# Diagonal products over both chunks of a unit in one matmul, with the results sorted on three engines

## What is computed

```python
x   = xBC[..., :D_INNER]                  # 64 heads x 16
Bm  = xBC[..., D_INNER:D_INNER + 512]     # 8 groups x 64 states
Cm  = xBC[..., D_INNER + 512:]
A_cum  = cumsum(A)                        # within a chunk
Lm     = exp(segsum(A))                   # decay from token z to token s of a chunk
Y_diag = einsum('bcshn,bczhn,bhcsz,bczhp->bcshp', Cm, Bm, Lm, X)
states = einsum('bcshn,bhcs,bcshp->bchpn', Bm, decay_states, X)
Y_off  = einsum('bcshn,bchpn,bhcs->bcshp', Cm, states, exp(A_cum))
y      = Y_diag + Y_off
out    = ((y + D * x / dt) * silu(z + z_bias)) @ out_proj_w.T
```

## Time and profile before

| | us |
|---|---|
| three runs | 672.77, 673.68, 674.39 |
| median | 673.68 |
| the profiled execution, whole | 675.71 |
| its span, first to last instruction | 674.0 |

### The profile page before, as it was taken

The page is one execution under the profiler, slowest core; times in us unless marked ns, Lnnn a source line. Parts: engine busy times, 40 slices in busy tenths (PEclk is TensorE's granted clock), DMA queues, the critical chain, the costliest instruction groups (busy, mean ns, idle before and its releaser), DMA issues.

```text
span 674.0 us, 21311 instructions
## 1 busy us (share of the span) xinstructions
PE 625.0 (93%) x8371; PEld 490.9 (73%) x8371; DVE 520.8 (77%) x947; ACT 383.7 (57%) x834; POOL 357.9 (53%) x416
## 2 busy tenths in 40 slices
PE   3786978999999999999999999999987989999995
PEld 1654856777877777778777777877866767888884
DVE  5799589788777786887878877787789466677766
ACT  3876453545756545665655565656665527665555
POOL 5775211535554554753644556356566746767652
PEclk9798788999999999999999999999998999999999
DMA  8743111142421231312122163221414634454411
GB/s 287 209 171 116 45 38 52 58 159 62 138 72 36 72 110 61 111 56 97 49 94 71 53 179 113 90 85 52 131 56 125 219 119 140 139 159 125 126 48 62
DMA packets 61914, 70.52 MB, mean 105 GB/s; under 512 B 13972, under 2 KB 33460, under 8 KB 61816
## 3 DMA queue, kind: packets, MB, share of 16 engines
q1 hardware_dynamic: 61816, 69.17, 32.2%
HBM read 54.45 MB, written 14.70 MB: 103 GB/s over the span
## 4 chain that ended last, share of the span: by engine, by line
PE 72%; DVE 12%; issue 4%; POOL 4%; ACT 3%; DMA 2%; SPq 1%; DVEq 0%; POOLq 0%; ACTq 0%
PE bank L1196 34%; PE bank L1963 11%; PE pair L1261 7%; PE bank L1205 4%; PE bank L1996 3%; PE pair L1234 3%; DVE m_cv L1447 2%; PE bank L1291 2%; PE bank L1214 2%; PE pair L1247 2%; DMA p_wa_raw<-in_L_attn_in_proj_w_dram 2%; DVE m_M L1477 1%; POOL h_lo L428 1%; DVE chain L589 1%; DVE chain L596 1%
## 5 line engine op out<-in xcount | busy, mean ns | idle before, releaser
L1447 DVE SCALAR_TENSOR_TENSOR m_cv<-bank,gpc,m_cv 128x511 f32<-128x511 f32 (+2 forms) x192 | 143.5, 748 | 35.5 <-ACT m_cv L1354 31.0
L1196 PE MATMUL bank<-h_hi,w_hi 128*128 128x512 f32 x384 | 160.8, 419 | 4.3 <-DVE m_xs L1468 2.1
L1196 PE MATMUL bank<-h_hi,w_lo 128*128 128x512 f32 x384 | 152.6, 397 | 0.0
L1196 PE MATMUL bank<-h_lo,w_hi 128*128 128x512 f32 x384 | 152.4, 397 | 0.0
L1592 POOL TENSOR_TENSOR m_S<-m_S,m_cd 128x128 f32<-128x128 f32 x96 | 39.9, 416 | 158.1 <-DVE m_S L1510 81.7
L1354 ACT ACTIVATE m_cv<-bank,gpc 128x512 f32<-128x512 f32 x96 | 72.0, 750 | 67.0 <-PE bank L1196 67.0
L1196 PEld LDWEIGHTS bank<-h_hi,w_hi 128*128 128x128 f32 x384 | 73.8, 192 | 24.0 <-issue 5.9
L1196 PEld LDWEIGHTS bank<-h_hi,w_lo 128*128 128x128 f32 x384 | 73.2, 191 | 16.9 <-issue 0.2
L1196 PEld LDWEIGHTS bank<-h_lo,w_hi 128*128 128x128 f32 x384 | 73.9, 192 | 13.7
L1366 ACT ACTIVATE m_M<-bank 128x512 f32<-128x512 f32 x128 | 76.2, 595 | 12.9 <-PE bank L1205 11.3
L1477 DVE TENSOR_TENSOR m_M<-m_M,pair 128x512 f32<-128x512 f32 x128 | 81.8, 680 | 0.2 <-issue 0.2
(11 more groups left out here) (184 smaller groups left out, 1271.9 us busy)
## 6 DMA issues: line engine op xcount, KB each, us to landing
m_ea<-ea_scratch SPq DMA_DIRECT2D x32, 256.0 KB
m_dd<-dd_scratch SPq DMA_DIRECT2D x32, 256.0 KB
y_scratch<-m_t SPq DMA_DIRECT2D x16, 512.0 KB, 3.4
h_lo_place<-y_scratch SPq DMA_DIRECT2D x16, 512.0 KB, 4.9
p_wm<-in_L_wmod_dram SPq DMA_DIRECT2D x6, 1024.0 KB, 7.7
m_wraw<-in_L_attn_in_proj_w_dram SPq DMA_DIRECT2D x18, 256.0 KB, 3.1
w_lo_place<-in_L_attn_input__dram SPq DMA_DIRECT2D x16, 256.0 KB, 5.0
out_dram<-t_o SPq DMA_DIRECT2D x16, 256.0 KB, 2.3
```

Source lines behind the costliest of these rows:

```text
L1196: ins = pe.matmul(A[k % 3][:, :], w[:, t, kc, :], h[:, n % NB, kc, :], start=(m == 0), stop=(m == 11))
L1447: ins = dve.scalar_tensor_tensor(out=cv[:, k % 3, lag:], in0=A[k % 3][:, 0:L - lag], scalar=s.gpc[:, gp, o:o + 1], in1=cv[:, k % 3, lag:], ...
```

## The change

A diagonal product now takes all 128 partitions, that is both chunks of a unit at once. Since the two chunks must not be added, a product handles head h of chunk 0 and the neighbouring head of the other parity of chunk 1: `Xp` holds x of chunk 1 at swapped places (`placed`), and the decay rows of chunk 1 are loaded with even and odd heads swapped, from a second scratch tensor `asw_d` in which SyncE stores them that way. So 16 products of 128 rows, 32 columns of weights and 64 moving columns take the place of 32 products of 64 rows. Their results go to columns 128 to 383 of `GB` (`OWN`), beside the turned B. In them even heads have their chunks in swapped order, odd heads in the right one. They are sorted by three engines: ScalarE copies them with the chunks swapped, times 1 on partitions of even heads and 0 on others (`even_heads`, a new instruction in slot 1), VectorE's `collect` adds them times the opposite mask, and GpSimd adds the even copy to `y1` (`add_even`, new). The masks (`s.parity`) are made once by six small GpSimd instructions. `spread` is two instructions of 64 partitions each, `weigh` two of 256 columns, the zeros included.

New waits: `turn_b(u)` waits for the collect of unit u-2, `diagonal(u)` for the copy of the B of unit u+1, `collect` for the even copy, and the sum of a step for `add_even`. `turn_b` moves ahead of the projection half of slot 3, and `exponent(u, 0)` ahead of `spread(u)`.

```diff
             def turn_b(u):
                 wait(pe, bt_read, u)
+                wait(pe, y1_done, u - 1)
                 pe.transpose(GB[:, 0:P], Bt[:, n % 2, tok(u)], s.ident[:, :]).then_inc(bt_done, 1)
...
             def diagonal(u):
                 wait(pe, y1_done, u)
+                pe.wait_ge(bt_read, min(u + 2, NU))
                 pe.wait_ge(s_new, n_new(u, 1))
                 pe.wait_ge(m_done, 2 * u + 2)
                 pe.wait_ge(xp_done, u + 1)
                 for q in range(2):
-                    for e in range(2):
+                    for a in range(2):
                         for j in range(4):
-                            for c in range(2):
-                                half, h = slice(64 * c, 64 * c + 64), 2 * j + e
-                                ins = pe.matmul(YS[32 * j:32 * j + 32, c, q * Q:(q + 1) * Q], Xp[half, u % 2, HG * q + h, :],
-                                                M[half, u % 2, q, h * Q:(h + 1) * Q], start=(e == 0), stop=(e == 1))
+                            h = 2 * j + a
+                            ins = pe.matmul(OWN[32 * j:32 * j + 32, q, (1 - a) * Q:(2 - a) * Q], Xp[:, u % 2, HG * q + h, :],
+                                            M[:, u % 2, q, h * Q:(h + 1) * Q], start=True, stop=True)
                 ins.then_inc(yd_done, 1)
...
                     if sl == 3 and u < NU:
                         decay(u, 1)
+                        turn_b(u)
                     if slot + 8 in PART_AT:
                         project(*PART_AT[slot + 8])
...
-                    if sl == 3 and u < NU:
-                        turn_b(u)
...
+            def even_heads(u):
+                act.wait_ge(yd_done, u + 1)
+                wait(act, y_added, u - 1)
+                act.activation(own_even[u % 2][:, :, :].rearrange("p q (c s) -> p q c s", c=2),
+                               OWN.rearrange("p q (c s) -> p q c s", c=2)[:, :, ::-1, :], ACT.Copy, scale=s.parity[:, 0:1]).then_inc(even_done, 1)
...
+                    if sl == 1 and v >= 0:
+                        even_heads(v)
...
                     if sl == 2 and u < NU:
+                        exponent(u, 0)
                         spread(u)
-                        exponent(u, 0)
...
-                dve.tensor_tensor(dst[:, first:, :, :], own[:, first:, :, :], dst[:, first:, :, :], ALU.add).then_inc(y1_done, 1)
+                dve.scalar_tensor_tensor(out=dst[:, :, first:], in0=OWN[:, :, first:], scalar=odd, in1=dst[:, :, first:],
+                                         op0=ALU.mult, op1=ALU.add).then_inc(y1_done, 1)
...
-                pool.tensor_tensor(Xw[:, :, :].rearrange("p q (j e d) -> p (q j) e d", e=2, d=HD), src, w, ALU.mult).then_inc(xw_done, 1)
+                for a in range(2):
+                    src, dst = (t[:, a::2, :].rearrange("p j (e d) -> p j e d", e=2) for t in (Xp[:, u % 2, :, :], Xw[:, :, :]))
+                    ins = pool.tensor_tensor(dst, src, w, ALU.mult)
+                ins.then_inc(xw_done, 1)
...
+            def add_even(u):
+                pool.wait_ge(y1_done, u + 1)
+                pool.wait_ge(even_done, u + 1)
+                y = y1[:, n % 2, :, tok(u)]
+                pool.tensor_tensor(y, y, own_even[u % 2][:, :, :], ALU.add).then_inc(y_added, 1)
...
                 if v + 2 < NU:
                     weigh(v + 2)
                     fade(v + 2, 0)
+                if v >= 0:
+                    add_even(v)
```

97 lines of the change are left out of this document (67 added, 30 removed).

## The result

The changed kernel takes **681.61 us** (median of four runs, 679.96 to 684.11) where the kernel before takes 673.22 beside it (671.30 to 674.39). The ratio is 1.0113, with a 95% interval of 1.0082 to 1.0143: slower by 1.1% (the two medians by themselves give 1.0125), where 666.0 was forecast. The profiled execution took 682.06 us with a span of 680.3.

What follows compares the result with a forecast made beforehand. TensorE's own stream was taken to bound the long middle (99.64 of 100 us busy). Terms -11.5 + 3.8 - 0.7 + 0.5 = -7.9 us from the 673.7 median gave 665.8, said as 666; range 660 to 673.

Steps and rivals of the forecast that it cites:

- The diagonal group: TensorE's diagonal products at a unit's head: 0.79 to 0.58 us, 0.21 less in 55 units, 11.5 us gained.
- Rivals B: Diagonal group shorter still, only its columns count: 0.44 us a unit, 661 us in all; chance 0.13.
- E: No gain in the diagonal group: a 128-row record costs twice a 64-row one, 0.79 stays, 677 us; chance 0.04.
- F: Weight loads show in each of the diagonal group's eight rounds, 0.13 us each, 725 us in all; chance 0.03.
- SyncE: Six small loads a unit instead of four, issued two units ahead (13 us): hidden, nothing counted, below 1 us otherwise.
- GpSimd: 1.2 us more a unit, 52% to 70% busy; TensorE waits 0.54 for the weighting in seven units, 3.8 us lost.
- The new wait of the turn of B on the collect: TensorE's turn of B waits for the collect of unit u-2: 1.4 us to spare in unit 29, nothing counted.
- The copy of B and VectorE's chain: Before the diagonal: chain about level, 0.5 us counted over the run; ScalarE's copy of B level, nothing counted.
- rivals C: VectorE's chain before the diagonal takes the gain back: odd units return about 0.2 us each, 671 to 672; chance 0.12.
- D: Diagonal waits for ScalarE's late copy of B: at 0.3 us a unit 16.5 us, 682 in all; chance 0.06.
- the sign that the prediction had named for itself: Unit 28 to unit 29, start to start, takes 6.46 us; wrong if it stays at 6.67 with a new idle stretch.
- The exponential ahead of the spread: ScalarE's first exponential no longer behind the 0.38 us spread, so TensorE's second decay product waits less: 0.7 us gained.

Runs made afterwards that it cites:

- run 1: Changed kernel with the six decay-row loads queued ahead of the store and scale loads on SyncE in a step's first unit; 1.0021 of the kernel before.
- run 5: Kernel before with only GpSimd's additional work put in from unit 8 on (second weighting, even-heads-sized add into a spare buffer); 1.0048, median 678.68 us.
- run 2: Changed kernel with GpSimd's new work taken away (half the weighting, one column of the even heads' sum), a test only; 0.9957 of the kernel before.
- run 4: Kernel of run 1 with, on GpSimd in a step's first unit, the weighting and fade ahead of the first gating; 0.9954 of the kernel before.
- run 8: Kernel of run 4 with the two y loads for the part behind the units issued ahead of decay rows and skips in unit 58; 668.87 us, 0.9902.
- run 3: Kernel before with the two moves alone: B turned sooner, first exponential ahead of spreading x; 0.9996 of the kernel before.
- run 6: Kernel before with the `Lm` load split in two by chunk, six decay-row loads a unit instead of four; 0.9985 of the kernel before.
- run 7: Kernel before with the decay-row loads queued ahead of the store and scale loads on SyncE; 0.9994 of the kernel before.
- run 10: Kernel before with the two y loads for the part behind the units issued ahead of decay rows and skips in unit 58; 0.9975.

## Why the prediction was wrong, point by point

- **The diagonal group**: right, 0.79 to 0.58 (300.71 to 301.29). Over 50 units the group alone gives -11.44, against the 11.5 of the term over 55: eleven of the 64 groups of the kernel before took 0.92 to 1.10 and not 0.79, so the size per unit is right and the total is helped by units that the forecast didn't look at. Rivals B (0.44) and E (0.79) fall. So does F: 32 records in 0.58 leave no room for a load of 0.13 in each of eight rounds, and the trace disagrees with the rule of the Trainium skill (TensorE: Matmul & The Clock Gate, Part 3: Packing small matmuls) as F had used it.
- **SyncE: this is the step that failed.** "Six small loads a unit instead of four, issued two units ahead of their use (13 us) ... Hidden, nothing counted." The 13 us hold for units in the middle of a step. In a step's first unit they stand behind the store, which waits for GpSimd: for unit 36's rows that left 3.9 us from the last issue to the use already in the kernel before (337.1 to 340.97), and 0.16 us from the landing. It is the wait of the decay product on these rows that was put at nothing. I priced the six loads by their own distance and never walked SyncE's queue past the store; the row that holds them, 333.48, was there to be read. Measured: +7.78 us, and -0.56 once the loads stand ahead of the store (run 1).
- **GpSimd**: "It has room except in one place." The place was right, and its price nearly: the states product waited from about 335.42 to 336.00 in unit 33, 0.58 where 0.54 was forecast, and the seven units that were named lost 3.3 us (0.37 to 0.58 each) where 3.8 was counted. Unit 7, which wasn't named, lost 1.1 more, which makes the 4.4. What was missing is the other reader of GpSimd in that unit: the store behind the second gating. 72% busy was no trouble; 1.26 us more ahead of one instruction was. Adding the even heads took 736 ns, not 0.62: the copy into a spare buffer in run 5, of the same columns, took 615.
- **The new wait of the turn of B on the collect**: right in the middle (1.4 to spare), wrong in the first steps, where VectorE does other work too: in unit 5 a reciprocal of 3.34 us stands ahead of the taps, the collect ends at 142.9, and the turn waits. Units 3 to 6 lost 3.2 in all; the forecast had looked at one unit for this wait. VectorE in unit 5:

```profile
135.76 3.34 DVE L652 RECIPROCAL chain<-chain 128x512 f32<-128x512 f32 x1
...
142.48 0.48 DVE L1548 SCALAR_TENSOR_TENSOR m_y<-bank,p_parity,m_y 128x256 f32<-128x256 f32 x1
```

and TensorE's row for that turn:

```profile
143.11 0.45 PE L1261 MATMUL bank<-ident,m_Bt 128*128 128x128 f32 x1 [2.10 <-DVE m_y L1548]
```

- **The copy of B and VectorE's chain** (rivals C and D): counted at 0.5, measured +1.35 in the changed kernel and +1.4 to +1.8 in runs 1, 2, 4 and 8. This is D's mechanism at about an eighth of D's price: in ten odd units between 7 and 45 the copy of B ended 0.10 us ahead of the diagonal group, which began 0.50 to 0.60 behind the last projection pass where 0.33 is usual, 2.2 us together. Unit 29 is one of them, at 307.37, and so the sign that the prediction had named for itself came out against it: unit 28 to unit 29 takes 6.66 us (300.71 to 307.37), where 6.46 was forecast and 6.67 stood before. The unit behind it has the 6.46. "Level again, nothing counted" was a little too hopeful. C's chain did not slip: the masked scores of these ten units were ready 0.49 us or more ahead of the group.
- **The exponential ahead of the spread**: 0.7 us can't be told (run 3, 0.9996; in its profile the piece from second decay to diagonal is -2.06, where runs 6, 7 and 10 have -0.2 to +0.2, so the two moves may well have given more, but the whole times don't show it).
- **The sum**: -7.9 was forecast for a kernel in which the decay rows are in time. Run 1 is that kernel, and its units 7 to 56 stand at -7.03. Units 0 to 6 give 4.2 of that back (the turn of B in unit 5 among it) and units 57 to 61 another 1.8, and its ratio is 1.0021. The sum was nearly right on the part of the program that it was read from and blind to the first units. The profile of run 1 is of a short execution, so these pieces don't add up to its ratio: some 4 us between that execution (a span 2.9 us shorter than before) and the ratio (1.4 us longer) stay unexplained.
- **The chances**: none of the rivals was the one that came. D, at 682, had the measured time with another cause: the numbers agree by chance. The 0.12 for slower was too little for a change that puts 1.3 us on an engine which gates a queue.

## What to carry to other kernels

Before an edit lengthens an engine's work, list everything that waits on each instruction behind it, and if one of these is a DMA issue, then everything queued behind that issue as well: "issued two units ahead" is only true of a queue that nobody holds. The distance from issue to use has to be read in the worst unit, not in a typical one. A small load that is needed soon doesn't belong behind a large store that waits for somebody: it waits for the store's release and then for its traffic. And the order of two fixes matters: moving the weighting forward cost 0.9% before the loads were moved, and gave 0.7% after.
